# A two-layer recurrent kernel: another order inside its last ten slots

## What is computed

```python
# first recurrence, 50 steps
z, r = sigmoid(xz + hz), sigmoid(xr + hr)
h = z * h + (1 - z) * tanh(xh + r * hh)
# attention score of every step: two relu layers on h, news and h * news
at = sigmoid(relu(relu(emb @ W1 + b1) @ W2 + b2) @ W3 + b3)
# second, gated recurrence over the same steps; its state is g in the kernel
u = sigmoid(h @ Wu + bu + g @ Uu)
r = sigmoid(h @ Wr + br + g @ Ur)
c = tanh(h @ Wc + bc + r * (g @ Uc))
g = g + at * u * (c - g)
# head on the last g and on news: batch norm, two dense layers, one output
```

## Time and profile before

| | us |
|---|---|
| median of 3 runs | 1911.99 |
| the profiled execution, own time | 1912.08 |
| its span | 1910.3 |
| TensorE matmul busy | 1893.0 |
| VectorE busy | 1542.7 |
| ScalarE busy | 1443.6 |
| GpSimd busy | 1635.7 |

### The profile page before, as it was taken

The page is one execution under the profiler, slowest core; times in us unless marked ns, Lnnn a source line. Parts: engine busy times, 40 slices in busy tenths (PEclk is TensorE's granted clock), DMA queues, the critical chain, the costliest instruction groups (busy, mean ns, idle before and its releaser), DMA issues. The chain is left out here.

```text
span 1910.3 us, 45939 instructions
## 1 busy us (share of the span) xinstructions
PE 1893.0 (99%) x17355; PEld 987.1 (52%) x17355; DVE 1542.7 (81%) x2401; ACT 1443.6 (76%) x2470; POOL 1635.7 (86%) x1391
## 2 busy tenths in 40 slices
PE   8999999999999999999999999999999999999998
PEld 4455555555555555555555555555555555555554
DVE  7899988878787877888787778878887877787776
ACT  7778777777777777777777777777777777777775
POOL 7789988888888888888888888888888888888873
PEclk9999999999999999999999999999999999999999
DMA  3211211121121112111211211121112111111100
GB/s 125 80 50 53 74 51 51 51 73 51 51 69 58 50 54 73 51 51 51 73 51 51 70 56 50 56 73 51 51 51 73 51 51 63 61 51 54 65 24 24
DMA packets 50259, 110.65 MB, mean 58 GB/s; under 512 B 16948, under 2 KB 17332, under 8 KB 43704
## 3 DMA queue, kind: packets, MB, share of 16 engines
q1 hardware_dynamic: 49960, 107.99, 17.9%
q10 hardware_dynamic: 144, 0.26, 0.1%
HBM read 107.39 MB, written 0.42 MB: 56 GB/s over the span
## 5 line engine op out<-in xcount | busy, mean ns | idle before, releaser
L1161 PE MATMUL ps<-h_hi,w_hi 128*64 128x512 f16 x1384 | 525.0, 379 | 7.2 <-DVE t L918 3.0
L1162 PE MATMUL ps<-h_hi,w_hi 128*64 128x512 f16 x1384 | 525.1, 379 | 0.0
L1162 PE MATMUL ps<-h_lo,w_hi 128*64 128x512 f16 x1384 | 524.6, 379 | 0.0
L1162 PE MATMUL ps<-h_hi,w_lo 128*64 128x512 f16 x1384 | 524.6, 379 | 0.0
L1161 PE MATMUL ps<-h_hi,w_lo 128*64 128x512 f16 x1384 | 524.6, 379 | 0.0
L1161 PE MATMUL ps<-h_lo,w_hi 128*64 128x512 f16 x1384 | 524.6, 379 | 0.0
L341 POOL TENSOR_TENSOR hn_lo<-hn,hn_hi 128x512 f16<-128x512 f32 x200 | 232.3, 1161 | 144.0 <-ACT hn_hi L483 144.0
L335 POOL TENSOR_TENSOR hn<-h,news 128x512 f32<-128x512 f32 x200 | 256.3, 1281 | 71.3 <-DVE h L1038 69.4
L628 ACT ACTIVATE ps<-gt,p_rest 128x512 f32<-128x512 f32 x185 | 127.7, 690 | 200.6 <-DVE gt L1035 200.5
L354 POOL TENSOR_TENSOR x_lo<-x,x_hi 128x512 f16<-128x512 f32 x196 | 228.6, 1167 | 19.1 <-ACT x_hi L503 15.0
L414 POOL TENSOR_TENSOR d<-h,hc 128x512 f32<-128x512 f32 x186 | 238.3, 1281 | 0.0
(11 more groups left out here) (176 smaller groups left out, 6826.0 us busy)
## 6 DMA issues: line engine op xcount, KB each, us to landing
score<-score_rows SPq DMA_DIRECT2D x50, 1024.0 KB, 4.7
x<-in_xs SPq DMA_DIRECT2D x199, 256.0 KB, 3.1
part_up<-part SPq DMA_DIRECT2D x100, 4.0 KB, 1.8
score_rows<-s_col SPq DMA_DIRECT2D x100, 4.0 KB, 1.4
news<-in_xs SPq DMA_DIRECT2D x4, 256.0 KB, 5.4
p_rest<-in_pack_rest SPq DMA_DIRECT2D x1, 776.0 KB, 7.6
p_att<-in_pack_att SPq DMA_DIRECT2D x1, 290.0 KB, 4.9
x<-in_xs ACTq DMA_DIRECT2D x1, 256.0 KB, 3.9
```

Source lines behind the costliest of these rows:

```text
L1161: m.matmul(ps[0:H, bank, :], weights[:, 0:H], moving, start=start, stop=stop)
L1162: return m.matmul(ps[H:P, bank, :], weights[:, H:P], moving, start=start, stop=stop)
```

## The change

Only the four `late` functions' order of work is touched, in three of them:

- TensorE does GR first, then GHH, then GU, then GXH. Before, GU came first in slots 201 to 209, and in slot 200 the order was GR, GU, GHH. `head_1_state(0)` of slot 208 still stands behind GR and ahead of GHH.
- ScalarE does the sigmoid gr as its first instruction of the slot. Before, it was last or nearly last.
- VectorE does reset times GHH (now line 1131) ahead of the difference, and the sum with GXH (now line 1117) between the gated step and the state. In slot 200 alone the sum comes behind the state. The attention's line 824 now follows all of that.

No instruction is added or removed, the same values are computed, and GpSimd's and the DMA queue's streams are the same.

```diff
@@ -702,6 +702,11 @@
 
             def late(low):
                 item = low - LAG
+                if low == LAST - 2:
+                    head_1(0)
+                if has(item):
+                    act.wait_ge(gr_pe, item - NC + 1)
+                    a.activation(gr[:, item % 2, :], ps[:, B_GR, :], ACT.Sigmoid, bias=b_gated[:, 1:2]).then_inc(gr_ready, 1)
                 if pairs_of(low - 1):
                     relu_2(0, ITEMS)
                     sign_2(0, ITEMS)
@@ -722,15 +727,10 @@
                     act.wait_ge(gu_pe, item + 1)
                     act.wait_ge(gus_ready, item - 1)
                     a.activation(gu[:, item % 2, :], ps[:, B_GU, :], ACT.Sigmoid, bias=b_gated[:, 0:1]).then_inc(gu_ready, 1)
-                if low == LAST - 2:
-                    head_1(0)
                 if low == ITEMS:
                     gated_high(item - 3)
                 if low <= SHORT:
                     gated_high(item - 2)
-                if has(item):
-                    act.wait_ge(gr_pe, item - NC + 1)
-                    a.activation(gr[:, item % 2, :], ps[:, B_GR, :], ACT.Sigmoid, bias=b_gated[:, 1:2]).then_inc(gr_ready, 1)
                 if SHORT <= low < LAST - 1:
                     gated_high(item - 1)
 
@@ -1109,31 +1109,37 @@
 
             def late(low):
                 item = low - LAG
+                k = item % 2
+
+                def candidate_sum():
+                    dve.wait_ge(gxh_pe, item + 1)
+                    dve.wait_ge(gt1_ready, item - NC + 1)
+                    v.tensor_tensor(gt[:, k, :], gt[:, k, :], ps[:, gxh_bank(item), :], ALU.add).then_inc(gt2_ready, 1)
+
                 if folds_of(low):
                     total_of(folded(low))
                 if pairs_of(low - 1):
                     sum_2(0, ITEMS)
                 if has(low - 2):
                     attention_1_news(low - 2, low - 1)
+                if low == LAST - 2:
+                    head_1(0, 0)
+                    head_1(0, 1)
+                if has(item):
+                    dve.wait_ge(ghh_pe, item - NC + 1)
+                    dve.wait_ge(gr_ready, item - NC + 1)
+                    v.tensor_tensor(gt[:, k, :], gr[:, k, :], ps[:, B_GHH, :], ALU.mult).then_inc(gt1_ready, 1)
                 gated_difference(item - 1, item)
                 if pairs_of(low - 1):
                     sum_2(1, ITEMS)
                 gated_step(item - 1, item)
+                if has(item) and low > ITEMS:
+                    candidate_sum()
                 gated_state(item - 1, item)
+                if low == ITEMS:
+                    candidate_sum()
                 if has(low - 2):
                     attention_1_low(low - 2, low - 1)
-                if low == LAST - 2:
-                    head_1(0, 0)
-                    head_1(0, 1)
-                if has(item):
-                    k = item % 2
-                    dve.wait_ge(ghh_pe, item - NC + 1)
-                    dve.wait_ge(gr_ready, item - NC + 1)
-                    v.tensor_tensor(gt[:, k, :], gr[:, k, :], ps[:, B_GHH, :], ALU.mult).then_inc(gt1_ready, 1)
-                if has(item):
-                    dve.wait_ge(gxh_pe, item + 1)
-                    dve.wait_ge(gt1_ready, item - NC + 1)
-                    v.tensor_tensor(gt[:, k, :], gt[:, k, :], ps[:, gxh_bank(item), :], ALU.add).then_inc(gt2_ready, 1)
                 if low == ITEMS:
                     shift_bias()
                 if low == ITEMS + 4:
@@ -1440,11 +1446,6 @@
                 hg = (h_hi[:, item % HIST, :], h_lo[:, item % HIST, :])
                 gg = (g_hi[:, item % NC, :], g_lo[:, item % NC, :])
 
-                def gated_update():
-                    split_product(B_GU, GW_U, *hg, start=True, stop=False)
-                    pe.wait_ge(glo_ready, item - NC + 1)
-                    split_product(B_GU, GU_U, *gg, start=False, stop=True).then_inc(gu_pe, 1)
-
                 if has(low - 2):
                     pe.wait_ge(a1lo_ready, low - 2)
                     attention_1(low - 2, low - 1)
@@ -1452,21 +1453,20 @@
                     pe.wait_ge(bn_ready, 3 * NEWTON + 6)
                     pe.wait_ge(t2_ready, ITEMS)
                     shift_product()
-                else:
-                    pe.wait_ge(gu_ready, item)
-                    gated_update()
                 pe.wait_ge(gr_ready, item - NC)
                 split_product(B_GR, GW_R, *hg, start=True, stop=False)
-                if low == ITEMS:
-                    pe.wait_ge(glo_ready, item - NC + 1)
+                pe.wait_ge(glo_ready, item - NC + 1)
                 split_product(B_GR, GU_R, *gg, start=False, stop=True).then_inc(gr_pe, 1)
-                if low == ITEMS:
-                    pe.wait_ge(h_ready, ITEMS)
-                    gated_update()
                 if low == ITEMS + LAG - 2:
                     head_1_state(0)
                 pe.wait_ge(gt1_ready, item - NC)
                 split_product(B_GHH, GU_C, *gg, start=True, stop=True).then_inc(ghh_pe, 1)
+                if low == ITEMS:
+                    pe.wait_ge(h_ready, ITEMS)
+                else:
+                    pe.wait_ge(gu_ready, item)
+                split_product(B_GU, GW_U, *hg, start=True, stop=False)
+                split_product(B_GU, GU_U, *gg, start=False, stop=True).then_inc(gu_pe, 1)
                 if low == ITEMS:
                     pe.wait_ge(g_ready, item)
                 elif low == ITEMS + 1:
```

## The result

| | before | changed |
|---|---|---|
| median, us | 1912.26 (1911.17 to 1913.03, 6 runs) | 1921.61 (1920.26 to 1923.78, 6 runs) |
| ratio, 95% interval | | 1.0052 (1.0042 to 1.0062) |
| profiled execution, own time | 1912.08 | 1920.26 |
| its span | 1910.3 | 1918.5 |

The change makes the kernel slower by 9.35 us, 0.5%. The forecast was 1919.4 in a range of 1916.2 to 1921.6: the direction is right, and the time is 2.2 us above the forecast, 0.01 us outside the range.

A forecast was written before the change was run, and what follows sets the result against it. TensorE, busy 99% of the span, was taken as the bound. New stalls of 10.1 us less 2.95 old gave +7.15, with small additions +7.4, so 1919.4 us; range 1916.2 to 1921.6.

The forecast's parts named there:

- the old ones: Six TensorE stalls in the tail of the kernel before, together 2.95 us, the most a better tail could win.
- small waits: First steps of the head, after slot 209: 0.3 us added for small TensorE waits.
- slot 200 for the state: Slot 200: TensorE's GXH of item 190 waits for the state of item 189, a stall of 1.8 us.
- `a_lo`: Slot 201: TensorE's attention waits for VectorE's `a_lo`, queued behind the sum of item 190, a stall of 1.55 us.
- `a_lo` before the second layer: Slot 201: TensorE's second attention layer waits for `a_lo` of item 199, a stall of 2.2 us.
- slot 203 together: Slot 203: TensorE's GHH and GU wait 0.2 us each, GXH 1.05; together 1.45 us.
- g_lo of item 196: Slot 208: TensorE reaches `head_1_state(0)` 1.3 us earlier in its slot and waits for g_lo, a stall of 1.6 us.
- gu of item 199: Near the head: TensorE's `head_1_news(1, 1)` waits for ScalarE's gu, a stall of 1.2 us.
- The list of signs: Expected profile signs, including longer idle in 1840 to 1860, `a_lo` waits, and no stall between 1864 and 1884.
- The gain: Slots 204 to 207: TensorE's 3.89 us per slot becomes the bound and stalls vanish; capped at 2.95 us.
- The ring: From slot 203, a VectorE and ScalarE dependency loop of 4.30 us; sum to sum would become 2.8 us.
- the third rival: TensorE's clock falls to 1.2 GHz behind a 2.2 us stall, adding 3.9 us, so 1923 us; chance 3%.

The follow-up runs named there:

- e2: Changed kernel with 7, 8 and 10 unneeded matmul pairs filling TensorE's three stalls of slots 200 and 201; median 1920.07 us, +7.2 against the kernel before.
- e7: Changed kernel with only the third stall (slot 201, before the second attention layer) filled with 10 matmul pairs; median +7.3 us against the kernel before.
- e8: Changed kernel with only the first two stalls (slots 200 and 201) filled with matmuls, the third left open; median +8.1 us against the kernel before.
- e11: Same kernel as e8, run again: changed kernel, first two stalls filled, third open; median +8.6 us against the kernel before.
- e12: Same kernel as e7, run again: changed kernel, only the third stall filled; median +10.4 us against the kernel before.
- e3: Changed kernel with `head_1_state(0)` of slot 208 behind GHH and GU instead of behind GR; median +7.0 us against the kernel before.
- e6: Changed kernel with relu and sign of the pair's first half ahead of the gr sigmoid on ScalarE in slot 202; median +8.8 us against the kernel before.
- e10: Changed kernel with VectorE's `a_lo` ahead of the sum with GXH and the state, behind the gated step; median +7.2 us against the kernel before.
- e5: Kernel before with the new order only in slots 203 to 206 (ScalarE, VectorE) and 204 to 206 (TensorE); median 1910.79 against 1912.18 us, ratio 0.9992.
- e1: The changed kernel run again without edit; median +8.3 us against the kernel before, five runs 1919.86 to 1921.57 us.
- e4: Changed kernel with slots 200 to 202 back in the old order on all three engines, new order from slot 203; 1915.09 against 1912.87 us before.
- e9: Kernel before with only TensorE in the new order, ScalarE and VectorE in the old one; median +6.9 us against the kernel before.

## Why the prediction was right, and where it was wrong

**The bound, right.** TensorE's stalls account for the time. With no fall of the clock the tail is 77.39 to 77.44 us (e2, e7, e8, e11, e12), which is 7.4 to 7.5 above the 69.97 of before; the forecast was +7.4. The new stalls add up to 10.10 and the old ones to 2.94, which leaves 7.16; from its first pair to the end the head takes 20.89 us before (from 1889.41) and 21.17 after (from 1897.33), the 0.3 that the forecast puts down for its small waits.

**The stalls, right one by one.** Forecast and measured: slot 200 for the state 1.8 and 1.86; `a_lo` 1.55 and 1.55; `a_lo` before the second layer 2.2 and 2.28; slot 203 together 1.45 and 1.53; g_lo of item 196 1.6 and 1.63; gu of item 199 1.2 and 1.25. e3, e6 and e10 each take one cause away and move the stalls that it was said to cause, by the amount that it was priced at; in e10 the fall of the clock hides some 0.2 of it. The list of signs contradicts this walk at one place: it asks for no stall between 1864 and 1884, where the walk itself has slot 203's wait for the state, which came at 1867.21.

**The gain, right, and given back.** The ring is gone, the three stalls that it made are gone (e5: the tail 1.95 us shorter). In the change it is paid for at both ends of the stretch: slots 200 to 202, where ScalarE and VectorE have other work that the early wait for GR holds up, and slots 208 and 209, where two products of cover were taken from in front of `head_1_state(0)` and three (GR's two and GHH) from behind the last GU.

**The clock, wrong.** The step that failed is the third rival and what I made of it. I gave it 3%, held against it that the clock stayed at 1.00 in a window with 1.28 us of idle time (the whole wait there is 1.56), and treated it as exclusive of the others. It is no alternative but comes on top of the forecast: all five profiles with the new order in slots 200 to 202 and nothing filled (change, e1, e3, e6, e10) have a fall, and none of the five with fillers has. The 1.56 us that stood against the fall are shorter than the 2.2 us walked, so the rows could not exclude the fall, and the range should have held it, from nothing to the whole slot. As it was, the range ended 1 us above a forecast without it. The size was off too: I priced one whole slot, +3.9; one fall in the profile cost 79.13 - 77.42 = 1.71 us, two 3.05, and single runs show groups 3.9 apart. With one or two falls in most executions the forecast would have been 1919.4 + 1.7 to 3.1, which is 1921.1 to 1922.5, and the measured 1921.61 lies in it. The Trainium skill, "TensorE: Matmul & The Clock Gate", section "What's actually happening", says that half the clock is the default and that activity releases it; the trace agrees, with a granted clock of 0.55 in 1855.5 to 1859.2 us of the changed kernel.

**The 0.2% bound, too coarse.** The prediction takes 3.8 us as the least that can be told from no change. With 11 runs against 15, e4's +2.2 us is told from it (ratio 1.0012, interval 1.0003 to 1.0021). The kernel before spreads over 2.0 us in 15 runs, and a part of that is the tail's start; the tail length is alike to 0.05 us between executions without a fall.

## What to carry to other kernels

Moving an instruction that waits for another engine to the front of an in-order stream makes everything behind it wait as well. It pays in the slots where that stream has nothing else to do, and costs wherever it does, so such a reordering is to be set slot by slot (e5), not for a whole phase. When an engine is busy for 99% of the time, add up both the gaps that an edit closes and those that it opens, and then ask whether the new ones are long or close enough together to slow the engine's clock as well.

## What the runs showed of the hardware

TensorE's clock fell from 2.4 to 1.2 GHz, in a part of the executions, behind stalls of 1.86 and 1.55 us with 0.65 us of matmuls between them (in the profiles of e3 and e6; in e7 and e12 by the times of single runs), and behind a single one of 2.32 us in a busy stretch (in the profile of e10; for 2.27 us in e11, two runs of five, by their times). The profiles of e8 and e11 have the single stall of 2.27 to 2.28 us and no fall. In the change and in e1, e3 and e6 it fell behind the third stall, of 2.28. It was not seen to fall behind single stalls of 1.62 (e4, eleven runs) nor behind four stalls of 1.39 us, each 3.9 us of work apart (e9, five runs). A fall cost 1.7 us in the profile of the change. Filling the stalls with matmuls that nobody needs kept the clock up and made the kernel shorter by about as much, 1.69 us of tail (e2).
